# Wide and narrow matmuls of neighbouring products put together in experts 1 to 7

## The chip, the cores and the metric

One core of one Trainium2 chip runs the whole kernel. The metric is the device time in microseconds (us): the median of three runs is 570.77 us (570.52 to 570.80). TensorE (PE) multiplies, VectorE (DVE) and ScalarE (ACT) prepare operands and read results out, GpSimd (POOL) and SyncE (SP) mainly issue transfers.

## The reference

A batch of 512 rows with 1024 features goes through eight experts of three layers, a softmax gate per task, and two small towers:

```python
h = relu(einsum('bi,eio->beo', x, eW1) + eb1)      # 8 experts, 1024 -> 1024
h = relu(einsum('beh,eho->beo', h, eW2) + eb2)     # 1024 -> 512
expert_out = einsum('beh,eho->beo', h, eW3) + eb3  # 512 -> 256
gates = softmax(einsum('bi,tie->bte', x, gW) + gb)
tin = einsum('bte,bed->btd', gates, expert_out)    # 2 tasks
th = relu(tin @ tW1 + tb1); th = relu(th @ tW2 + tb2)   # per task
out = sigmoid(th @ tW3 + tb3)
```

Everything is float32, and the result has to be near float32.

## The kernel before

**Precision.** Each float32 operand is split into a high part (a rounding that PE can read in one pass, `fp32r`) and a low part, the rest. ACT writes the high parts (`w_hi`), DVE the low parts (`w_lo` = raw minus high). A product is then high x high + high weights x low data + low weights x high data. In layers 2 and 3 and the towers these are three matmuls of 512 columns (`triple`, L379 to L382; L380, L381, L382 in the profile).

**Layer 1.** Experts 1 to 7 and half of expert 0 compute layer 1 by a Strassen-Winograd scheme with seven products, P1 to P7, in place of eight. The 1024 outputs are cut into four pairs of two column blocks of 128 (pair 0 to 3). For each pair, `product` (L524) runs one product: four *wide* matmuls (L537: weights `w_hi`, moving data the high and low halves of x or of a sum of x blocks, 2 x 256 = 512 columns), then four *narrow* ones (L540: weights `w_lo`, 256 columns). The last narrow one raises the semaphore `slot_used`, so whoever waits for the product or for its weight slot waits for its narrow part.

**Order on PE.** `pair(e, i)` (L544) gives P1, P2, P5, P6, then P4 of the pair before, P3, P7. Between them stand waits: P6 waits until ACT has copied P1's sum out of PSUM (`n1_taken`, L570), P4 waits for `lower_summed` (L589), P3 until ACT has copied P5 (`p5_taken`, L578), P7 until ACT has copied P6 (`n2_taken`, L582). After pair 3 come layer 3 of the expert before (`layer3`, 24 matmuls; its second half waits for `upper_done` of pair 3, L644), P4 of pair 3, and layer 2 (96 matmuls). PE, ACT and DVE each have this program as a hardware loop over experts 1 to 6, and once more unrolled for expert 7 (`LAST`), where pair 3 is followed by layer 2 at once.

**Order on ACT.** ACT works strictly in its written order (L980 to L1025). The lines that matter are
- `g1_hi` (L822): high parts of the weights of P1, P2, P5 of one pair; `g3_hi` (L850) those of P3 and P7; `g4_hi` (L857) that of P4, into a slot that an earlier product must have left
- `n1_take` (L864), `n2_take` (L871), `p5_take` (L878): the copies out of PSUM of the sums after P1, P6, P5; `p5_take` also waits for `lower_done`
- `c21_take` (L889): reads the result of P4; `pair_h1` (L894): the pair's hidden values.

In pair 0 the order is `g4_hi(0)`, `n1_take(0)`, `g1_hi(1)`, `p5_take(0)`, `g3_hi(1)`, `n2_take(0)`; in pair 2 it is `n1_take(2)`, `p5_take(2)`, `g4_hi(2)`, `g1_hi(3)`, `n2_take(2)`, `c21_take(1)`.

**Order on DVE.** DVE too keeps its written order (L1399 to L1464). `g4_lo(2)`, `sum2(3)`, `sum4(3)`, `g1_lo(3)` follow each other; `g1_lo(3)` releases P1 of pair 3 (`slot_ready`). After `g4_lo(3)` come `c12_sum(2)` (L1213), `upper_fold(2)` (L1228), `lower_fold(2)` (L1241, releases `lower_done`), `c11_sum(3)` (L1207), `w3_lo`, `c21_fold(2)` (L1247, waits for `c21_take(2)`), `w2_lo(0)`, `pair_h1_lo(2)` (L1156, waits for ACT's `pair_h1(2)`), `c12_sum(3)`, `upper_fold(3)`. Low parts of weights are all on L1140.

Of the kernel before, what the change touches and what calls it, by code (L numbers as in the profile page):

```python
# [13 lines left out]
P = 128  # L14
# [68 lines left out]
FIRST_PAIR = 2  # L83
# [62 lines left out]
def nth(e, i):  # L146

    return PAIRS * (e - 1) + i + (PAIRS - FIRST_PAIR)
# [36 lines left out]
def slot_of(product):  # L185
    return USER[product] % RING


def moe_towers(nc, xT, eW1_first, eW1_pairs, eW2, eW3, tW1, tW2, small, out):
    with ExitStack() as ctx:  # L190
# [12 lines left out]
        w_hi, w_lo = sb("w_hi", [RING, SLOT], F32R), sb("w_lo", [RING, SLOT], F32R)  # L203
# [10 lines left out]
        banks = [psum[:, b * BATCH:(b + 1) * BATCH] for b in range(8)]  # L214
# [60 lines left out]
        def halved(x):  # L275
            return x.rearrange("p (n b) -> p n b", n=2)
# [209 lines left out]
        def _(pe):  # L486
# [34 lines left out]
                        pe.matmul(banks[BANK_GROUP[m]][:], w[:, PIECE_SLOT[0], m * P:(m + 1) * P], x[:, 0, :],  # L521
                                  start=(n == 0), stop=False)

            def product(e, p, i):  # L524
                bank_of_pair, source, kh, xh, starts, ends = PRODUCTS[p]
                slot = slot_of((p, i))
                whole = halved(banks[bank_of_pair[i]])
                both = x_both if source == "x" else t_both

                def weights(w, kk):  # L530
                    return w[:, slot, kk * P:(kk + 1) * P]

                def moving(kk):
                    return both[:, :, kh * KK + kk, xh * HALF:(xh + 1) * HALF]

                for kk in range(KK):
                    pe.matmul(whole, weights(w_hi, kk), moving(kk), start=(starts and kk == 0), stop=False,  # L537
                              skip_group_check=True)
                for kk in range(KK):
                    mm = pe.matmul(whole[:, 0, :], weights(w_lo, kk), moving(kk)[:, 0, :], start=False,  # L540
                                   stop=(ends and kk == KK - 1), skip_group_check=True)
                mm.then_inc(slot_used, 1)

            def pair(e, i):  # L544
                first = isinstance(e, int) and e == 0

                if i == PAIRS - 1 and not first:
                    pe.wait_ge(combined, nth(e, 0) + 1)
                elif i == 1:
                    pe.wait_ge(h2_staged, K3 * e)  # L550
                pe.wait_ge(slot_ready, split(e, "G0" if first else "G1", i))
                product(e, "P1", i)

                if not first and i >= 2:
                    pe.wait_ge(upper_done, nth(e, i) - 1)
                elif first and i == FIRST_PAIR:
                    pe.wait_ge(logitsT_ready, 1)
                elif first:
                    pe.wait_ge(h1_staged, 2)
                product(e, "P2", i)  # L560
                if first:
                    pe.wait_ge(slot_ready, split(e, "G1", i))
                    if i == FIRST_PAIR:
                        pe.wait_ge(t_ready, 1)
                if i == 0:

                    pe.wait_ge(gated_ready, 1 + GATED * (e - 1))
                product(e, "P5", i)

                pe.wait_ge(n1_taken, nth(e, i) + 1)  # L570
                pe.wait_ge(slot_ready, split(e, "G2", i))
                if first and i == FIRST_PAIR:
                    pe.wait_ge(t_ready, 2)
                product(e, "P6", i)
                if i > (FIRST_PAIR if first else 0):
                    last_product(e, i - 1)

                pe.wait_ge(p5_taken, nth(e, i) + 1)  # L578
                pe.wait_ge(slot_ready, split(e, "G3", i))
                product(e, "P3", i)  # L580

                pe.wait_ge(n2_taken, nth(e, i) + 1)  # L582
                if first and i == FIRST_PAIR:
                    pe.wait_ge(t_ready, NX)
                product(e, "P7", i)

            def last_product(e, i):

                pe.wait_ge(lower_summed, nth(e, i) + 1)  # L589
                pe.wait_ge(slot_ready, split(e, "G4", i))  # L590
                if isinstance(e, int) and e == 0:
                    pe.wait_ge(t_ready, NX)
                product(e, "P4", i)

            def layer2(e):
                first, last = isinstance(e, int) and e == 0, isinstance(e, int) and e == LAST
# [123 lines left out]
            for k, t in by_tile(range(KT1), T):  # L720
                pe.wait_ge(slot_ready, split(LAST, "T1", t))
                pe.wait_ge(tin_ready, T * k + t + 1)
                for m in range(KT2):
# [4 lines left out]
                    if k == 0 and t == 1:  # L728
# [3 lines left out]
                    slot, cols = TOWER_SLOT["T1", t] + k, slice(m * P, (m + 1) * P)  # L732
                    mm = triple(pe, banks[bank][:], w_hi[:, slot, cols], w_lo[:, slot, cols],
                                x_hi[:, t * OUT3 + k, :], x_lo[:, t * OUT3 + k, :], k == 0, k == KT1 - 1)
# [8 lines left out]
            for t in range(T):  # L743
                pe.wait_ge(slot_ready, split(LAST, "T2", t))
                for i, (k, m) in enumerate(by_bank(range(KT2), KT1)):
# [4 lines left out]
                    if k == 0:  # L750

                        pe.wait_ge(tower1_staged, 2 * t + m + 1)
                    mm = triple(pe, halved(banks[BANK_TOWER2[t][m]]), *tower2_weights(t, k, m),
                                h1_hi[:, :, t * KT2 + k, :], h1_lo[:, :, t * KT2 + k, :], k == 0, k == KT2 - 1)
# [3 lines left out]
            for h in range(2):  # L758
                pe.wait_ge(tower1_staged, 2 * t + m + 1 + h)
                for k in range(KT2):  # L760
                    mm = triple(pe, banks[BANK_LAST[h]][:, 0:HALF], *tower2_weights(t, k, m),
                                h1_hi[:, h, t * KT2 + k, :], h1_lo[:, h, t * KT2 + k, :], k == 0, k == KT2 - 1)
# [4 lines left out]
            for n, (t, cols) in enumerate([(0, slice(0, BATCH)), (1, slice(0, HALF)), (1, slice(HALF, BATCH))]):  # L767
                pe.wait_ge(folded, n + 1)
                pe.matmul(banks[BANK_FINAL[n]][0:1, cols], ones[:], tail_out[:, t * KT1, cols],  # L769
                          start=True, stop=True).then_inc(final_done, 1)  # L770
# [363 lines left out]
        def _(dve):  # L1134
# [63 lines left out]
            def g4_lo(e, i):  # L1198
                first = slot_of(("P4", i))
                split_lo(split(e, "G4", i), slice(first, first + 1), raw_block(i, A22))  # L1200
# [8 lines left out]
            def c12_sum(e, i):  # L1209

                dve.wait_ge(n2_taken, nth(e, i) + 1)
                dve.wait_ge(slot_used, used(e, ("P3", i)))
                dve.tensor_tensor(upper[:, 1, :, :], halved(banks[Q_BANK[i]]), upper[:, 1, :, :],  # L1213
                                  ALU.add).then_inc(upper_summed, 1)
# [22 lines left out]
            def lower_fold(e, i):  # L1237

                quarter_free(e, i)
                dve.wait_ge(lower_summed, nth(e, i) + 1)  # L1240
                dve.scalar_tensor_tensor(quarter[:, 3, :], lower[:, 0, :], prm_of("b1", e * K2 + MG + i),  # L1241
                                         lower[:, 1, :], ALU.add, ALU.add).then_inc(lower_done, 1)
# [156 lines left out]
            with dve.Fori(1, LAST) as e:  # L1399
                sum2(e, 0)  # L1400
                g1_lo(e, 0)
                sum4(e, 0)
                g2_lo(e, 0)
                g3_lo(e, 0)
                hidden2_lo(e, 0)
                hidden2_lo(e, 1)
                hidden2_lo(e, 2)
                g4_lo(e, 0)
                sum2(e, 1)
                sum4(e, 1)  # L1410
                g1_lo(e, 1)
                g3_lo(e, 1)
                c11_sum(e, 0)
                c22_sum(e, 0)
                g2_lo(e, 1)
                hidden2_lo(e, 3)
                lower_fold(e, 0)
                c12_sum(e, 0)
                c11_sum(e, 1)
                g4_lo(e, 1)  # L1420
                upper_fold(e, 0)
                sum2(e, 2)
                sum4(e, 2)
                g1_lo(e, 2)
                c21_fold(e, 0)
                c12_sum(e, 1)
                g2_lo(e, 2)
                c22_sum(e, 1)
                pair_h1_lo(e, 0)
                upper_fold(e, 1)  # L1430
                lower_fold(e, 1)
                g3_lo(e, 2)
                c11_sum(e, 2)
                g4_lo(e, 2)
                sum2(e, 3)
                sum4(e, 3)
                g1_lo(e, 3)
                c21_fold(e, 1)
                g2_lo(e, 3)
                c22_sum(e, 2)  # L1440
                pair_h1_lo(e, 1)
                g3_lo(e, 3)
                g4_lo(e, 3)
                c12_sum(e, 2)
                upper_fold(e, 2)
                lower_fold(e, 2)
                c11_sum(e, 3)
                w3_lo(e)
                c21_fold(e, 2)
                w2_lo(e, 0)  # L1450
                pair_h1_lo(e, 2)
                c12_sum(e, 3)
                upper_fold(e, 3)
                c22_sum(e, 3)
                gate_output(e, 0)
                lower_fold(e, 3)
                w2_lo(e, 1)
                c21_fold(e, 3)
                gate_output(e, 1)
                pair_h1_lo(e, 3)  # L1460
                w2_lo(e, 2)
                w2_lo(e, 3)
                gate_output(e, 2)
                gate_output(e, 3)  # L1464

            e = LAST
# [41 lines left out]
            pair_h1_lo(e, 1)  # L1508
            g3_lo(e, 3)
            g4_lo(e, 3)  # L1510
            c12_sum(e, 2)
            upper_fold(e, 2)
            lower_fold(e, 2)
            c11_sum(e, 3)
            w2_lo(e, 0)
            c21_fold(e, 2)
# [189 lines left out]
```

## Time and profile before

| | us |
|---|---|
| median of three runs | 570.77 |
| the profiled execution | 571.16 |
| its span, first to last instruction | 569.4 |
| PE matmuls busy | 565.6 (99%) |
| DVE busy | 453.8 (80%) |
| ACT busy | 311.1 (55%) |
| TensorE clock granted | 1.000 of full speed |

The busy time of PE counts every matmul from its start to its modelled end, and neighbouring ones overlap. The distance from one start to the next is what a matmul costs in a stream; the timeline gives it. The third expert of the loop is taken as the example below: its P1 of pair 0 starts at 205.28 us.

### The profile page before, as it was taken

The numbers are of one execution on the slowest core, as the hardware profiler recorded it, in microseconds if no ns is written. First come the engines' busy times: TensorE is split into PE (matmuls) and PEld (weight loads), VectorE is DVE, ScalarE is ACT, GpSimd is POOL, SyncE is SP. The second block draws the span as 40 slices with busy tenths as digits, with TensorE's granted clock in tenths as the row PEclk, the third lists the DMA queues.
The fourth block names the chain that finished last, engine by engine and source line by source line (L and its number), as shares of the span: only waits on it lengthen the run. The fifth ranks groups of instructions, "written<-read, shape, count | busy, mean of one in ns | idle before, by whom it ended". The sixth has DMA issues, their size and how long they took to land.

```text
span 569.4 us, 8432 instructions
## 1 busy us (share of the span) xinstructions
PE 565.6 (99%) x2883; PEld 477.6 (84%) x2883; DVE 453.8 (80%) x580; ACT 311.1 (55%) x422; POOL 93.8 (16%) x102
## 2 busy tenths in 40 slices
PE   9999999999999999999999999999999999999998
PEld 6788888888888888888888888888888888888886
DVE  7998579975997769976799759978699767986795
ACT  3584566535663375733665356633757346663644
POOL 0201311052102411033200431024110331100000
PEclk9999999999999999999999999999999999999999
DMA  9727676467726675466744577266654667535000
GB/s 329 212 62 218 151 225 144 147 162 180 178 77 184 189 163 128 147 166 172 197 101 163 145 200 178 79 181 192 161 129 147 166 171 199 149 130 185 0 1 1
DMA packets 39779, 86.94 MB, mean 153 GB/s; under 512 B 3521, under 2 KB 8769, under 8 KB 39762
## 3 DMA queue, kind: packets, MB, share of 16 engines
q1 hardware_dynamic: 29762, 66.50, 34.7%
q0 software_dynamic: 9856, 19.96, 20.9%
q10 hardware_dynamic: 144, 0.26, 0.2%
q8 instruction: 9, 0.15, 0.1%
q14 instruction: 8, 0.07, 0.0%
HBM read 86.68 MB, written 0.04 MB: 152 GB/s over the span
## 4 chain that ended last, share of the span: by engine, by line
PE 98%; ACT 1%; DVE 0%; issue 0%; ACTq 0%
PE psum L537 34%; PE psum L540 17%; PE psum L380 15%; PE psum L381 15%; PE psum L382 15%; PE psum L701 1%; PE psum L521 1%; PE psum L678 0%; ACT scratch L790 0%; ACT scratch L1130 0%; PE psum L769 0%; DVE h_lo L1156 0%; DVE w_lo L1140 0%; ACT w_hi L835 0%; PE psum L687 0%
## 5 line engine op out<-in xcount | busy, mean ns | idle before, releaser
L1140 DVE TENSOR_TENSOR w_lo<-w_raw,w_hi 128x1024 fp32r<-128x1024 f32 (+2 forms) x108 | 135.5, 1255 | 26.3 <-ACT w_hi L857 12.3
L537 PE MATMUL psum<-t_both,w_hi 128*128 128x512 f32 x480 | 130.8, 394 | 0.0
L380 PE MATMUL psum<-h_hi,w_hi 128*128 128x512 f32 (+1 forms) x332 | 128.6, 387 | 0.0
L381 PE MATMUL psum<-h_lo,w_hi 128*128 128x512 f32 (+1 forms) x332 | 128.5, 387 | 0.0
L382 PE MATMUL psum<-h_hi,w_lo 128*128 128x512 f32 (+1 forms) x332 | 128.3, 387 | 0.0
L537 PE MATMUL psum<-x_both,w_hi 128*128 128x512 f32 x360 | 98.2, 394 | 0.0
L537 PEld LDWEIGHTS psum<-t_both,w_hi 128*128 128x128 f32 x480 | 82.6, 189 | 11.5
L1626 POOL DMA_DIRECT2D w_raw<-eW_pairs x30 | 26.0, 868 | 344.8 <-DMA w_raw<-eW_pairs 344.8
L540 PEld LDWEIGHTS psum<-t_both,w_lo 128*128 128x128 f32 x480 | 73.7, 189 | 10.2
L1140 DVE TENSOR_TENSOR w_lo<-scratch,w_hi 128x512 fp32r<-128x512 f32 (+1 forms) x60 | 57.1, 952 | 24.4 <-ACT w_hi L850 23.8
L540 PE MATMUL psum<-t_both,w_lo 128*128 128x256 f32 x480 | 76.4, 281 | 0.0
L1156 DVE SCALAR_TENSOR_TENSOR h_lo<-scratch,h_hi 128x512 fp32r<-128x512 f32 (+1 forms) x62 | 63.3, 1022 | 15.1 <-ACT scratch L930 12.3
L382 PEld LDWEIGHTS psum<-h_hi,w_lo 128*128 128x128 f32 x332 | 62.4, 188 | 12.8
L380 PEld LDWEIGHTS psum<-h_hi,w_hi 128*128 128x128 f32 x332 | 62.4, 188 | 12.3
L381 PEld LDWEIGHTS psum<-h_lo,w_hi 128*128 128x128 f32 x332 | 62.4, 188 | 12.1
L537 PEld LDWEIGHTS psum<-x_both,w_hi 128*128 128x128 f32 x360 | 62.1, 189 | 8.8
L540 PEld LDWEIGHTS psum<-x_both,w_lo 128*128 128x128 f32 x360 | 55.2, 189 | 7.6
L540 PE MATMUL psum<-x_both,w_lo 128*128 128x256 f32 x360 | 57.2, 281 | 0.0
L850 ACT ACTIVATE w_hi<-scratch 128x1024 fp32r<-128x1024 f32 x30 | 31.5, 1051 | 32.0 <-PE psum L382 32.0
L822 ACT ACTIVATE w_hi<-w_raw 128x1536 fp32r<-128x1536 f32 x28 | 41.5, 1483 | 13.1 <-PE psum L382 13.1
L894 ACT ACTIVATE h_hi<-scratch 128x1024 fp32r<-128x1024 f32 x30 | 31.8, 1061 | 22.0 <-DVE scratch L1247 22.0
L918 ACT ACTIVATE w_hi<-w_raw 128x1024 fp32r<-128x1024 f32 x32 | 33.5, 1049 | 17.8 <-DMA w_raw<-eW 16.7
(109 smaller groups left out, 605.3 us busy)
## 6 DMA issues: line engine op xcount, KB each, us to landing
w_raw<-eW_pairs SPq DMA_DIRECT2D x30, 768.0 KB, 4.2
w_raw<-eW SPq DMA_DIRECT2D x40, 512.0 KB, 3.9
scratch<-eW_pairs SPq DMA_DIRECT2D x30, 256.0 KB, 4.9
w_raw<-eW_pairs SPq DMA_DIRECT2D x30, 256.0 KB, 5.1
w_raw<-eW_pairs POOLq DMA_DIRECT2D x30, 256.0 KB, 5.0
scratch<-eW_pairs POOLq DMA_DIRECT2D x30, 256.0 KB, 6.5
scratch<-gates_dram POOLq DMA_DIRECT2D x8, 512.0 KB, 5.6
w_raw<-tW SPq DMA_DIRECT2D x4, 512.0 KB, 4.2
```

The lines of the kernel that those rows point to most:

```text
L380: pe.matmul(bank, weights_hi, moving_hi, start=first, stop=False)
L381: pe.matmul(bank, weights_hi, moving_lo, start=False, stop=False)
L382: return pe.matmul(bank, weights_lo, moving_hi, start=False, stop=last)
L537: pe.matmul(whole, weights(w_hi, kk), moving(kk), start=(starts and kk == 0), stop=False, skip_group_check=True)
L540: mm = pe.matmul(whole[:, 0, :], weights(w_lo, kk), moving(kk)[:, 0, :], start=False, stop=(ends and kk == KK - 1), skip_group_check=True)
L822: act.activation(wide(slice(first, first + 3)), raw_block(i, A11, 3), ACT.Copy).then_inc(slot_hi, 1)
L850: act.activation(wide(slice(first, first + 2)), sums[:, at:at + 2, :].rearrange("p s w -> p (s w)"), ACT.Copy).then_inc(slot_hi, 1)
L894: act.activation(pair_of(h1_hi, i), quarter[:], ACT.Relu).then_inc(h1_taken, 1)
L918: act.activation(wide(slice(2 * i, 2 * i + 2)), unit(u), ACT.Copy).then_inc(slot_hi, 1)
L1140: dve.tensor_tensor(wide(w_lo, slots), raw, wide(w_hi, slots).bitcast(F32), ALU.subtract).then_inc(slot_ready, 1)
L1156: return dve.scalar_tensor_tensor(lo, staged, 0.0, hi.bitcast(F32), ALU.max, ALU.subtract)
L1626: pool.dma_start(raw_block(i, A21), blocks_dram(e, i, A22), accum_op=ALU.add) \
```

## The change

`product` is cut into `high` (the four wide matmuls) and `low` (the four narrow ones with the `slot_used` increment). In experts 1 to 7 the wide parts of two neighbouring products run first, then their narrow parts: P1 with P2 in every pair, P5 with P6 in pairs 1 to 3, and P4 (of the pair before) with P3 in pairs 1 to 3. P7, P5, P6 and P3 of pair 0, P4 of pair 3 and all of expert 0 keep their form. The narrow parts finish in the same sequence as before. The waits stand ahead of the wide part of the product that they guard. On DVE, `lower_fold(2)` moves ahead of `c12_sum(2)` and `upper_fold(2)`, in the loop and in the last expert.

```diff
-                product(e, "P1", i)
+                high("P1", i)
+                if first:
+                    low("P1", i)
                 if not first and i >= 2:
                     pe.wait_ge(upper_done, nth(e, i) - 1)
...
-                product(e, "P2", i)
+                high("P2", i)
+                if not first:
+                    low("P1", i)
+                low("P2", i)
...
-                product(e, "P5", i)
+                high("P5", i)
+                if first or i == 0:
+                    low("P5", i)
                 pe.wait_ge(n1_taken, nth(e, i) + 1)
                 pe.wait_ge(slot_ready, split(e, "G2", i))
...
-                product(e, "P6", i)
-                if i > (FIRST_PAIR if first else 0):
-                    last_product(e, i - 1)
+                high("P6", i)
+                if not first and i > 0:
+                    low("P5", i)
+                low("P6", i)
+                with_last = i > (FIRST_PAIR if first else 0)
+                if with_last:
+                    wait_last(e, i - 1)
+                    high("P4", i - 1)
+                    if first:
+                        low("P4", i - 1)
                 pe.wait_ge(p5_taken, nth(e, i) + 1)
                 pe.wait_ge(slot_ready, split(e, "G3", i))
-                product(e, "P3", i)
+                high("P3", i)
+                if with_last and not first:
+                    low("P4", i - 1)
+                low("P3", i)
...
                 g4_lo(e, 3)
+                lower_fold(e, 2)
                 c12_sum(e, 2)
                 upper_fold(e, 2)
-                lower_fold(e, 2)
                 c11_sum(e, 3)
```

## Rows read from the trace of the kernel before

**Rows 1.** The page, part 4: engines' shares of the chain that ended last.
```profile
PE 98%; ACT 1%; DVE 0%; issue 0%; ACTq 0%
```
**Rows 2.** Waits of PE: engine, line, releaser: us in total, times, longest.
```profile
PE psum L701 <- DVE scratch L1297: 1.2, 1, 1.2
PE psum L687 <- ACT scratch L790: 0.3, 1, 0.3
```
**Rows 3.** Timeline of PE, the third looped expert: start us, us, engine, line, operation.
```profile
205.28 1.07 PE L537 MATMUL psum<-x_both,w_hi 128*128 128x512 f32 x4
...
206.66 1.09 PE L537 MATMUL psum<-x_both,w_hi 128*128 128x512 f32 x4
...
223.50 1.09 PE L537 MATMUL psum<-x_both,w_hi 128*128 128x512 f32 x4
...
227.23 0.63 PE L540 MATMUL psum<-t_both,w_lo 128*128 128x256 f32 x4
...
233.32 1.09 PE L537 MATMUL psum<-x_both,w_hi 128*128 128x512 f32 x4
...
243.14 0.40 PE L380 MATMUL psum<-h_hi,w_hi 128*128 128x512 f32 x1
...
245.89 0.39 PE L380 MATMUL psum<-h_hi,w_hi 128*128 128x512 f32 x1
...
248.61 1.07 PE L537 MATMUL psum<-t_both,w_hi 128*128 128x512 f32 x4
249.52 0.64 PE L540 MATMUL psum<-t_both,w_lo 128*128 128x256 f32 x4
249.99 0.40 PE L380 MATMUL psum<-h_hi,w_hi 128*128 128x512 f32 x1
...
271.78 0.39 PE L537 MATMUL psum<-x_both,w_hi 128*128 128x512 f32 x1
```
**Rows 4.** Timeline of PE, narrow triples of the last layer (same columns).
```profile
562.49 0.28 PE L382 MATMUL psum<-h_hi,w_lo 128*128 128x256 f32 x1
...
562.85 0.28 PE L382 MATMUL psum<-h_hi,w_lo 128*128 128x256 f32 x1
```
**Rows 5.** Timeline of ACT, that expert's pair 0; brackets: idle before, releaser.
```profile
206.85 0.63 ACT L857 ACTIVATE w_hi<-w_raw 128x512 fp32r<-128x512 f32 x1 [1.37 <-PE psum L540]
...
207.87 1.48 ACT L822 ACTIVATE w_hi<-w_raw 128x1536 fp32r<-128x1536 f32 x1
209.66 0.60 ACT L878 ACTIVATE scratch<-psum 128x512 f32<-128x512 f32 x1 [0.31 <-PE psum L540]
```
**Rows 6.** Timeline of ACT, pair 2.
```profile
227.90 0.60 ACT L878 ACTIVATE scratch<-psum 128x512 f32<-128x512 f32 x1 [2.21 <-PE psum L540]
228.40 0.62 ACT L857 ACTIVATE w_hi<-w_raw 128x512 fp32r<-128x512 f32 x1
```
**Rows 7.** Timeline of DVE, pair 2.
```profile
229.05 0.69 DVE L1140 TENSOR_TENSOR w_lo<-w_raw,w_hi 128x512 fp32r<-128x512 f32 x1 [0.40 <-ACT w_hi L857]
...
230.99 1.75 DVE L1140 TENSOR_TENSOR w_lo<-w_raw,w_hi 128x1536 fp32r<-128x1536 f32 x1
```
**Rows 8.** Timeline of ACT, pair 3.
```profile
239.15 0.60 ACT L878 ACTIVATE scratch<-psum 128x512 f32<-128x512 f32 x1 [1.14 <-PE psum L540]
```
**Rows 9.** Timeline of DVE, pair 3 and layer 3.
```profile
238.58 0.48 DVE L1241 SCALAR_TENSOR_TENSOR scratch<-scratch,prm 128x256 f32<-128x256 f32 x1
...
241.22 0.42 DVE L1247 TENSOR_TENSOR scratch<-scratch,psum 128x256 f32<-128x256 f32 x1 [0.44 <-ACT scratch L889]
...
244.75 0.75 DVE L1228 SCALAR_TENSOR_TENSOR scratch<-scratch,prm 128x512 f32<-128x512 f32 x1
```
**Rows 10.** Timeline of all engines where PE was held in expert 0.
```profile
37.52 0.71 ACT L790 ACTIVATE scratch<-psum,prm 128x512 f32<-128x512 f32 x1
...
38.37 0.63 PE L687 MATMUL psum<-ident,scratch 128*128 128x128 f32 x4 [0.28 <-ACT scratch L790]
...
38.75 0.48 PE L537 MATMUL psum<-x_both,w_hi 128*128 128x512 f32 x1
```

More of the change, by code:

```diff
@@ L522, in first_tile, with of_product, high, low @@
                                   start=(n == 0), stop=False)
-            def product(e, p, i):
+            def of_product(p, i):
                 bank_of_pair, source, kh, xh, starts, ends = PRODUCTS[p]
-                slot = slot_of((p, i))
-                whole = halved(banks[bank_of_pair[i]])
                 both = x_both if source == "x" else t_both
-                def weights(w, kk):
-                    return w[:, slot, kk * P:(kk + 1) * P]
                 def moving(kk):
                     return both[:, :, kh * KK + kk, xh * HALF:(xh + 1) * HALF]
+                return slot_of((p, i)), halved(banks[bank_of_pair[i]]), moving, starts, ends
+            def high(p, i):
+                slot, whole, moving, starts, ends = of_product(p, i)
                 for kk in range(KK):
-                    pe.matmul(whole, weights(w_hi, kk), moving(kk), start=(starts and kk == 0), stop=False,
+                    pe.matmul(whole, w_hi[:, slot, kk * P:(kk + 1) * P], moving(kk), start=(starts and kk == 0), stop=False,
                               skip_group_check=True)
+            def low(p, i):
+                slot, whole, moving, starts, ends = of_product(p, i)
                 for kk in range(KK):
-                    mm = pe.matmul(whole[:, 0, :], weights(w_lo, kk), moving(kk)[:, 0, :], start=False,
+                    mm = pe.matmul(whole[:, 0, :], w_lo[:, slot, kk * P:(kk + 1) * P], moving(kk)[:, 0, :], start=False,
                                    stop=(ends and kk == KK - 1), skip_group_check=True)
                 mm.then_inc(slot_used, 1)
+            def product(p, i):
+                high(p, i)
+                low(p, i)
             def pair(e, i):
@@ L584, in pair, with wait_last @@
                     pe.wait_ge(t_ready, NX)
-                product(e, "P7", i)
-            def last_product(e, i):
+                product("P7", i)
+            def wait_last(e, i):
                 pe.wait_ge(lower_summed, nth(e, i) + 1)
@@ L592, in last_product @@
                     pe.wait_ge(t_ready, NX)
-                product(e, "P4", i)
+            def last_product(e, i):
+                wait_last(e, i)
+                product("P4", i)
             def layer2(e):
@@ L1510, in _ @@
             g4_lo(e, 3)
+            lower_fold(e, 2)
             c12_sum(e, 2)
             upper_fold(e, 2)
-            lower_fold(e, 2)
             c11_sum(e, 3)
```

## The prediction

> **What bounds the kernel now.** I read the shares of the chain first: PE holds 98% of it [rows 1]. Then the waits of PE: two in the whole run, 1.5 us together, both outside the experts that change [rows 2]. So today no copy, split or load holds PE; time is the number of matmuls times their distance. Two questions follow: does the new order alter the distances, and do the waits between products stay covered. For the first I read PE's timeline, for the second those of ACT and DVE beside it.
>
> **Distances.** In layer 3 and layer 2 a 512-column matmul comes every 0.227 us. In a stream of narrow ones the distance is 0.120 (0.36 for three [rows 4]). Four wide and four narrow at these rates would be 1.387 us. P4 of pair 3, which follows layer 3, takes 1.38 (248.61 to 249.99), and so does P1 of pair 0 (205.28 to 206.66). But the 26 products from 206.66 to 243.14 take 36.48, 1.403 each [rows 3]. So a return from narrow to wide costs about 17 ns. The price is paid by the wide matmuls that follow: the 12 matmuls from 243.14 to 245.89 take 2.75, where 12 x 0.227 is 2.72 [rows 3].
>
> **What the grouping gives back.** One merged pair of products is 8 wide and 8 narrow: 8 x 0.227 + 0.95 + 0.03 for the return = 2.79, against 2 x 1.403 = 2.81. That is 14 ns each, if eight narrow ones leave no larger debt than four. If the debt goes by the number of narrow matmuls it is nothing. If each removed return saves its full mean it is 17. There are 10 merges per expert, 70 in all: 0 to 1.2 us, and I take 1.0 as long as PE is never held.
>
> The Trainium skill, page "TensorE: Matmul & The Clock Gate", section "Back-to-back issue gap", gives a warm distance of columns / 2.4 + 2.5 ns, 216 and 109 ns here, with no term for the order. By it the regrouping gives exactly 0. The trace disagrees, with 227 and 120 ns and 17 ns per return; I go by the trace.
>
> **What the grouping moves.** A product's `slot_used` rises after its narrow part. In a merged pair the second product ends when it did before. The first one (P1, P5, P4) now ends after both wide parts and its own narrow one, so 4 wide matmuls, 0.9 us, later. At the same time the second product's wide part, and the wait ahead of it, comes 0.47 earlier. Everything queued behind a wait for P1, P5 or P4 on ACT moves by 0.9, and what DVE builds on it too. I follow the four places where a wait of PE has little slack, in the expert that starts at 205.28. Three prices are used: a PE result reaches ACT 0.31 after the start of the last narrow matmul (206.54, which is 206.66 less 0.12, to 206.85 [rows 3, 5]); DVE starts about 0.04 after ACT; and ACT and DVE start an instruction about 0.10 before the one before it ends (227.90 + 0.60 to 228.40 [rows 6]). For the restart of PE after a wait the rows have one case: ACT ends at 38.23, the matmul starts at 38.37, and the next wide one takes 0.48 instead of 0.40 [rows 10]. That is 0.14 to 0.22. I take 0.17, with 0.08 and 0.24 as ends.
>
> *1. P3 of pair 0.* P1 now ends its narrow part later: last narrow start 205.28 + 8 x 0.227 + 0.35 = 207.44, before 206.54. `g4_hi(0)` waits for P1's slot and starts at 207.75 instead of 206.85 [rows 5]. Behind it `n1_take(0)` and `g1_hi(1)` follow at once, so `p5_take(0)` starts 1.02 + 1.48 - 0.10 = 2.40 later, at 210.15, and ends at 210.75. Today it had 0.31 idle ahead of it, so it moves by 0.5 only. P3 would start at 205.28 + 2.77 + 2.80 = 210.85. 210.75 + 0.17 is 210.92: held 0.07 (0 to 0.14). P7 behind it has its `n2_take(0)` just in time. The P1 and P2 block saves 0.02, so pair 1 starts 0.05 late.
>
> *2. Pair 1.* `n1_take`, `p5_take` and `g1_hi(2)` each move by about 0.9 against the pair's start and stay ahead of PE by 0.35 or more. The three merges save 0.04.
>
> *3. P1 of pair 3.* This one is the chain that I trust most. P5 of pair 2 had its last narrow start 4.09 after the pair's start (three products less 0.12); now it is 2.80 + 8 x 0.227 + 0.35 = 4.99, so 0.90 later. `p5_take(2)` waited for P5, and `g4_hi(2)` starts right behind it [rows 6]. DVE's `g4_lo(2)` waited 0.40 for that `g4_hi`, and `sum2(3)`, `sum4(3)` and `g1_lo(3)` follow it without a gap, to 232.74 [rows 7]. No idle time is left in this chain to take up 0.90, so `g1_lo(3)` ends at 233.64. P1 of pair 3 starts at 233.32 today, 0.58 behind its weights [rows 3]. Now: 233.64 + 0.17 = 233.81, so 0.49 late (0.40 to 0.56).
>
> *4. The second half of layer 3.* P4 of pair 2 had its last narrow start 6.90 after pair 3's start; now it is 2.80 + 2.79 + 1.81 + 0.35 + a return of 0.03 = 7.78, or 0.88 later. `c21_take(2)` waits for it, `c21_fold(2)` waited 0.44 for that, then come ACT's `pair_h1(2)`, `pair_h1_lo(2)`, `c12_sum(3)` and `upper_fold(3)`, each bound by the one before, to 245.50 [rows 9]. The second half of layer 3 starts at 245.89 [rows 3] and waits for that fold. Now 245.50 + 0.88 + 0.17 = 246.55: 0.66 late (0.57 to 0.73). Expert 7 has no layer 3 there, and the waits of its layer 2 that depend on pair 3 come 5 us later.
>
> **The fold that is moved** removes one such case. `p5_take(3)` waits for `lower_fold(2)`: that ends at 239.06, and `p5_take(3)` starts at 239.15 [rows 8, 9]. With the later `g4_lo(3)` and the old order it would end 6.8 us after the pair's start, where P3 needs it by 6.35. In the new order the fold is done by 4.7, and ACT's own queue sets `p5_take(3)`, at 5.4 to 6.0. Its price is 0.4 us on `upper_fold(2)`, whose readers (`n2_take(3)`, layer 3) come later than that. DMA: the loads that SP issues after a split move by up to 1 us too. They are issued some microseconds ahead of their use and I cost them at nothing; without that cover it would be at most that 1 us per expert.
>
> **Sum.** Later per expert: 0.05 - 0.04 + 0.49 + 0.66 = 1.16 us, six times 7.0. Expert 7: 0.05 - 0.04 + 0.49 - 0.04 = 0.46. Together +7.4 us, with the ends at (0.91 x 6 + 0.3) = 5.8 and (1.41 x 6 + 0.7) = 9.2. The profiled execution took 571.16, 0.4 above the median, so the same sum on the median 570.77 gives 578.2 (576.6 to 580.0). The gain of the grouping all but vanishes in it: from P1 of pair 3 on, PE starts when it is released and not when it is free.
>
> **Rivals.**
> - *All waits stay covered.* Then the order of matmuls alone speaks: 570.77 - 1.0 = 569.8, or 569.6 with the full 17 ns. For it: PE has no wait today. Against it: two chains without idle time, 0.58 and 0.39 ahead of PE, moved by 0.9. It is the case on the other side, and it decides from the point where each release comes less than 0.4 later than today; past that the waits eat the 1.0 at once. 8%, of which most is faster.
> - *The order doesn't matter and the waits stay covered*, as the page's rule has it for the matmuls: 570.8. The 17 ns in the rows speak against it. 3%.
> - *Only one of the two chains bites.* If layer 3 is not held (`upper_fold(3)` in time), 7.4 - 6 x 0.70 = 3.2, so 574.0; if P1 of pair 3 is not held, 7.4 - 7 x 0.53 = 3.7, 574.5. For it: each chain has five links that I take as rigid. 7%.
> - *A knock-on.* P3 of pair 3 has 0.34 of slack after `p5_take(3)`. If `w2_hi(0)` or `w3_split` ahead of it on ACT waits for its load, or P7 of pair 0 and pair 2 are held 0.1 each, another 0.2 to 0.9 per expert: 580 to 584. 7%.
>
> The forecast itself has 75%. As range I take 574.5 to 580.5. Faster by over 0.2% (1.1 us, about what a measurement of this kernel can tell from no change) has 6%, within 0.2% 5%, slower 89%.
>
> **What the changed profile would show.** PE's waits should list a line of `high` behind DVE `w_lo` seven times with about 0.5, and L380 behind DVE's `upper_fold` six times with about 0.6 to 0.7. The period from one looped expert's P1 to the next, 66.50 today (205.28 to 271.78 [rows 3]), should be near 67.66. `p5_take(2)` should start 5.3 after its pair, not 4.4. A merged block should take 2.79; 2.81 would say that the debt goes by narrow matmuls. The prediction is wrong if the period is below 66.6 or if PE is held in pair 3 at P3.

## The result, and the profile after

The changed kernel takes 579.16 us (median of 4 runs, 578.88 to 579.50) against 570.78 in the same comparison: ratio 1.0143, 95% interval 1.0131 to 1.0155, so 8.4 us slower. 578.2 was forecast, with a range of 574.5 to 580.5. The profiled execution took 579.38, its span is 577.6, and the TensorE clock was again 1.000.

The shares of the chain that ended last, and the waits of PE (engine, line, releaser: us in total, times, longest), of the kernel after:

```profile
PE 87%; DVE 6%; issue 4%; ACT 2%; ACTq 0%; DVEq 0%
```

```profile
PE psum L380 <- DVE scratch L1257: 2.5, 6, 0.4
PE psum L538 <- DVE w_lo L1169: 1.5, 7, 0.3
PE psum L730 <- DVE scratch L1326: 1.2, 1, 1.2
PE psum L716 <- ACT scratch L819: 0.3, 1, 0.3
```

The share of PE in that chain falls from 98% [rows 1] to 87%, while DVE goes from 0% to 6%, "issue" from 0% to 4% and ACT from 1% to 2%. The two old waits of PE are still there (1.2 and 0.3 [rows 2]). Two are new, one six times and one seven times: L380, the triple of layer 3, behind DVE's L1257 (`upper_fold`), and L538, a wide part, behind DVE's L1169 (low parts of weights). The totals of 2.5 and 1.5 us are only the time in which PE had nothing in flight, so they are smaller than the loss. That is read from the starts. PE's timeline after, third looped expert (it starts at 207.94, before at 205.28):

```profile
207.94 1.98 PE L538 MATMUL psum<-x_both,w_hi 128*128 128x512 f32 x8
209.75 1.11 PE L545 MATMUL psum<-x_both,w_lo 128*128 128x256 f32 x8
210.70 1.09 PE L538 MATMUL psum<-t_both,w_hi 128*128 128x512 f32 x4
...
213.53 1.19 PE L538 MATMUL psum<-x_both,w_hi 128*128 128x512 f32 x4
...
216.44 2.00 PE L538 MATMUL psum<-x_both,w_hi 128*128 128x512 f32 x8
...
219.23 2.00 PE L538 MATMUL psum<-t_both,w_hi 128*128 128x512 f32 x8
...
226.22 2.02 PE L538 MATMUL psum<-x_both,w_hi 128*128 128x512 f32 x8
...
229.02 2.00 PE L538 MATMUL psum<-t_both,w_hi 128*128 128x512 f32 x8
...
234.60 1.16 PE L538 MATMUL psum<-t_both,w_hi 128*128 128x512 f32 x4
...
236.42 2.14 PE L538 MATMUL psum<-x_both,w_hi 128*128 128x512 f32 x8 [0.20 <-DVE w_lo L1169]
...
239.34 2.00 PE L538 MATMUL psum<-t_both,w_hi 128*128 128x512 f32 x8
...
246.32 0.40 PE L380 MATMUL psum<-h_hi,w_hi 128*128 128x512 f32 x1
...
249.66 0.50 PE L380 MATMUL psum<-h_hi,w_hi 128*128 128x512 f32 x1 [0.41 <-DVE scratch L1257]
...
252.56 1.07 PE L538 MATMUL psum<-t_both,w_hi 128*128 128x512 f32 x4
...
275.72 0.62 PE L538 MATMUL psum<-x_both,w_hi 128*128 128x512 f32 x2
```

The times in the next sentences are counted from the start of the expert, and those of before from [rows 3]. The wide part of P1 of pair 3 begins at 28.48, before at 28.04; the second half of layer 3 at 41.72, before at 40.61; the next expert at 67.78, before at 66.50. Over the six looped experts the mean period is 67.74 (from 72.48 to 478.91), so +1.24 each. A merged block takes 2.79 to 2.80 (216.44 to 219.23, where the P5/P6 block begins, and 226.22 to 229.02), the one that follows the wide matmuls of layer 2 takes 2.76 (207.94 to 210.70), and eight narrow ones take 0.95 (209.75 to 210.70).

ACT after, pair 0 and pair 2:

```profile
210.42 0.63 ACT L886 ACTIVATE w_hi<-w_raw 128x512 fp32r<-128x512 f32 x1 [2.27 <-PE psum L545]
...
212.82 0.59 ACT L907 ACTIVATE scratch<-psum 128x512 f32<-128x512 f32 x1
```

```profile
231.53 0.60 ACT L907 ACTIVATE scratch<-psum 128x512 f32<-128x512 f32 x1 [2.19 <-PE psum L545]
232.02 0.62 ACT L886 ACTIVATE w_hi<-w_raw 128x512 fp32r<-128x512 f32 x1
```

`g4_hi(0)` starts 2.48 after the expert, before 1.57 [rows 5]. `p5_take(0)` has no idle time left ahead of it and ends at 213.41, 0.12 before P3's wide part (213.53). `p5_take(2)` starts 5.31 after its pair, before 4.40 [rows 6].

DVE after, pair 2:

```profile
232.68 0.69 DVE L1169 TENSOR_TENSOR w_lo<-w_raw,w_hi 128x512 fp32r<-128x512 f32 x1 [0.77 <-ACT w_hi L886]
...
234.62 1.75 DVE L1169 TENSOR_TENSOR w_lo<-w_raw,w_hi 128x1536 fp32r<-128x1536 f32 x1
```

`g4_lo(2)` waits 0.77 where it waited 0.40 [rows 7]. The chain behind it is as dense as before and ends at 236.37. PE starts P1 at 236.42.

ACT and DVE after, pair 3 and layer 3:

```profile
241.97 0.58 ACT L907 ACTIVATE scratch<-psum 128x512 f32<-128x512 f32 x1
...
244.82 0.47 ACT L918 ACTIVATE scratch<-psum,prm 128x256 f32<-128x256 f32 x1 [1.33 <-PE psum L545]
```

```profile
240.82 0.48 DVE L1270 SCALAR_TENSOR_TENSOR scratch<-scratch,prm 128x256 f32<-128x256 f32 x1
...
245.33 0.42 DVE L1276 TENSOR_TENSOR scratch<-scratch,psum 128x256 f32<-128x256 f32 x1 [0.80 <-ACT scratch L918]
...
248.86 0.75 DVE L1257 SCALAR_TENSOR_TENSOR scratch<-scratch,prm 128x512 f32<-128x512 f32 x1
```

`lower_fold(2)` now runs at 240.82, before `p5_take(3)` at 241.97, and no releaser stands beside `p5_take(3)`; before, they stood 0.09 apart [rows 8, 9]. P7 of pair 2 (234.60) takes 1.16 for its wide part where an unheld one takes 1.09: ACT's `n2_take(2)`, the copy that it waits for, ends only 0.10 ahead of it. `c21_take(2)` (L918) starts 8.40 after pair 3, before 7.40 (at 240.72 in that trace). `c21_fold(2)` waits 0.80 for it where it waited 0.44 [rows 9], and `upper_fold(3)` ends at 249.61. The second half of layer 3 starts at 249.66.

### The profile page after: what moved, and what is told of

It reads as the page before. It is cut to its first block, busy times and chain, and to the rows that moved or that the text cites. A ratio compares the mean times of both kernels' runs of the same rounds, so it can differ in the third digit from the quotient of the medians.

```text
span 577.6 us, 8432 instructions
## 1 busy us (share of the span) xinstructions
PE 569.8 (99%) x2883; PEld 478.7 (83%) x2883; DVE 452.1 (78%) x580; ACT 310.3 (54%) x422; POOL 93.7 (16%) x102
## 3 DMA queue, kind: packets, MB, share of 16 engines
q1 hardware_dynamic: 29762, 66.50, 34.1%
## 4 chain that ended last, share of the span: by engine, by line
PE 87%; DVE 6%; issue 4%; ACT 2%; ACTq 0%; DVEq 0%
PE psum L538 29%; PE psum L380 14%; PE psum L381 14%; PE psum L382 14%; PE psum L545 14%; DVE w_lo L1169 4%; DVE scratch L1206 1%; DVE scratch L1257 1%; ACT w_hi L886 1%; DVE scratch L1242 1%; PE psum L730 1%; PE psum L521 1%; ACT scratch L918 1%; PE psum L707 0%; ACT scratch L819 0%
## 5 line engine op out<-in xcount | busy, mean ns | idle before, releaser
L1169 DVE TENSOR_TENSOR w_lo<-w_raw,w_hi 128x1024 fp32r<-128x1024 f32 (+2 forms) x108 | 135.2, 1253 | 40.0 <-ACT w_hi L886 21.3
L380 PE MATMUL psum<-h_hi,w_hi 128*128 128x512 f32 (+1 forms) x332 | 129.2, 389 | 2.5 <-DVE scratch L1257 2.5
L538 PE MATMUL psum<-t_both,w_hi 128*128 128x512 f32 x480 | 127.5, 394 | 0.0
L538 PE MATMUL psum<-x_both,w_hi 128*128 128x512 f32 x360 | 94.3, 396 | 1.5 <-DVE w_lo L1169 1.5
L538 PEld LDWEIGHTS psum<-t_both,w_hi 128*128 128x128 f32 x480 | 84.1, 189 | 12.9
L538 PEld LDWEIGHTS psum<-x_both,w_hi 128*128 128x128 f32 x360 | 65.2, 188 | 15.9 <-DVE w_lo L1169 2.5
L545 PEld LDWEIGHTS psum<-t_both,w_lo 128*128 128x128 f32 x480 | 70.7, 189 | 8.1
L1169 DVE TENSOR_TENSOR w_lo<-scratch,w_hi 128x512 fp32r<-128x512 f32 (+1 forms) x60 | 57.1, 951 | 25.0 <-ACT w_hi L879 24.6
L380 PEld LDWEIGHTS psum<-h_hi,w_hi 128*128 128x128 f32 x332 | 62.4, 188 | 17.1 <-DVE scratch L1257 5.0
L545 PE MATMUL psum<-t_both,w_lo 128*128 128x256 f32 x480 | 72.9, 281 | 0.0
L545 PE MATMUL psum<-x_both,w_lo 128*128 128x256 f32 x360 | 52.8, 281 | 0.0
L545 PEld LDWEIGHTS psum<-x_both,w_lo 128*128 128x128 f32 x360 | 50.0, 190 | 3.4
L918 ACT ACTIVATE scratch<-psum,prm 128x256 f32<-128x256 f32 x30 | 14.2, 474 | 54.8 <-PE psum L545 54.8
```

Of the source, the lines that this page charges most:

```text
L380: pe.matmul(bank, weights_hi, moving_hi, start=first, stop=False)
L538: pe.matmul(whole, w_hi[:, slot, kk * P:(kk + 1) * P], moving(kk), start=(starts and kk == 0), stop=False, skip_group_check=True)
L545: mm = pe.matmul(whole[:, 0, :], w_lo[:, slot, kk * P:(kk + 1) * P], moving(kk)[:, 0, :], start=False, stop=(ends and kk == KK - 1), skip_ ...
L918: act.activation(quarter[:, 1, :], halved(banks[N_BANK[i]])[:, 0, :], ACT.Identity, bias=bias, scale=-1.0).then_inc(c21_taken, 1)
L1169: dve.tensor_tensor(wide(w_lo, slots), raw, wide(w_hi, slots).bitcast(F32), ALU.subtract).then_inc(slot_ready, 1)
```

## The experiments

Two theories stood against each other. By the *release theory* the loss is made by the later end of the first product of a merged block, in three places of which each belongs to one kind of block. By the *matmul theory* the blocks of eight are dearer on PE in themselves. All ratios are to the kernel before on the same chip, which took 571.00 us beside the first four kernels and 571.05 beside the last three. The period is the time from P1 of one looped expert to P1 of the next, 66.50 in the kernel before.

**One kind of block at a time.** The same edit for each of the three, with the other two kinds in their old form. Three small functions say of each kind whether it is merged; in each kernel one of them is always true and the other two are false. The later `low` of each block, not shown, gets the opposite condition:

```diff
-                if first:
+                if first or not merge12(e, i):
                     low("P1", i)
...
-                if first or i == 0:
+                if first or i == 0 or not merge56(e, i):
                     low("P5", i)
...
-                    if first:
+                    if first or not merge43(e, i):
                         low("P4", i - 1)
```

*P1 and P2 only.* 

> Only P1 and P2 are put together (28 blocks in seven experts); P5/P6 and P4/P3 keep their old form, the fold stays moved. Release theory (the loss is the later end of the first product of a merged block): only P3 of pair 0 is held, 0.12 us in each of seven experts, less 28 x 0.014: +0.4 us, 571.2. Matmul theory (blocks of eight are dearer in themselves, 8.4 us over 70 blocks): 28 x 0.12 = +3.4, 574.1, with no hold in the waits of PE.

Measured: 571.31 us, ratio 1.0009 (0.9999 to 1.0018). PE's timeline of this kernel, third looped expert:

```profile
204.95 1.98 PE L538 MATMUL psum<-x_both,w_hi 128*128 128x512 f32 x8
...
210.55 1.19 PE L538 MATMUL psum<-x_both,w_hi 128*128 128x512 f32 x4
...
271.54 0.84 PE L538 MATMUL psum<-x_both,w_hi 128*128 128x512 f32 x3
```

The period is 66.59, 0.09 over that of before. P3 of pair 0 begins 5.60 after the expert. Its four wide matmuls take 1.19, where a group that isn't held takes 1.09: the first distance is 0.10 longer. The list of waits has nothing new in the experts, since matmuls of the product before are still in flight. That is the release theory's size, and the whole +0.3 us lies near the noise of the runs; the matmul theory is 2.8 us off.

*P5 and P6 only.* 

> Only P5 and P6 are put together in pairs 1 to 3 (21 blocks). Release theory: P5 of pair 2 ends 0.9 later, P1 of pair 3 is held by g1_lo(3) in seven experts, 0.55 each, layer 3 is not held: 3.8 - 0.3 = +3.5, 574.3. Matmul theory: 21 x 0.12 = +2.5, 573.3, without a hold.

Measured: 574.50, ratio 1.0062 (1.0045 to 1.0078). The waits of PE:

```profile
PE psum L538 <- DVE w_lo L1178: 1.5, 7, 0.3
PE psum L739 <- DVE scratch L1335: 1.2, 1, 1.2
PE psum L538 <- ACT scratch L916: 0.9, 1, 0.9
PE psum L725 <- ACT scratch L828: 0.3, 1, 0.3
```

The wait of L538 behind DVE is there seven times, and the one of L380 is not. (The 0.9 behind ACT is in expert 0; see the last section.) The period is 67.00, +0.50.

*P4 and P3 only.* 

> Only P4 and P3 are put together in pairs 1 to 3 (21 blocks). Release theory: P4 of pair 2 ends 0.9 later, the second half of layer 3 is held by upper_fold(3) in six experts and not in expert 7, 0.66 each, P1 of pair 3 is not held: 4.0 - 0.3 = +3.7, 574.5. Matmul theory: +2.5, 573.3, without a hold and the same in expert 7.

Measured: 575.10, ratio 1.0077 (1.0061 to 1.0094). The waits of PE:

```profile
PE psum L380 <- DVE scratch L1266: 2.5, 6, 0.4
PE psum L739 <- DVE scratch L1335: 1.2, 1, 1.2
PE psum L725 <- ACT scratch L828: 0.3, 1, 0.3
```

Here L380 waits six times, for `upper_fold`, and L538 never. The period is 67.23, +0.73, and in expert 7 the time from its P1 to its layer 2 is 37.83, where it was 37.86. The matmul theory would have put the same cost there. The three parts add 0.3 + 3.5 + 4.1 = 7.9 us, against 8.4 for all together.

**The fold put back.** The changed kernel with the old order on DVE:

```diff
                 g4_lo(e, 3)
-                lower_fold(e, 2)
                 c12_sum(e, 2)
                 upper_fold(e, 2)
+                lower_fold(e, 2)
```

> The changed kernel with lower_fold(2) put back behind upper_fold(2). If the moved fold covers P3 of pair 3, as forecast: lower_fold(2) ends 1.5 us later, p5_take(3) ends 0.9 later and P3 of pair 3 is held 0.66 in seven experts, with all behind it: +4.6, 583.8. If the fold is off the path: 579.2 as the changed kernel.

Measured: 583.38, ratio 1.0220 (1.0203 to 1.0237), 4.2 us over the changed kernel (4.0 if each is set against the kernel before beside it), and a period of 68.41, 0.67 over that of the changed kernel. ACT and PE, pair 3 of an expert that starts at 208.52:

```profile
243.44 0.60 ACT L907 ACTIVATE scratch<-psum 128x512 f32<-128x512 f32 x1 [0.82 <-DVE scratch L1270]
```

```profile
244.17 1.18 PE L538 MATMUL psum<-x_both,w_hi 128*128 128x512 f32 x4 [0.39 <-ACT scratch L907]
```

`p5_take(3)` idles 0.82 behind L1270, `lower_fold`, and P3 of pair 3 is held behind it; the list of waits has L538 behind L907 seven times, once per changed expert. So the moved fold does cover that place.

**The fold alone**, the same move in the kernel before: 

> The kernel before with only lower_fold(2) moved ahead of c12_sum(2). In the kernel before P3 of pair 3 had 0.6 us of slack behind p5_take(3) and PE had no wait; the move gives slack and takes 0.4 from upper_fold(2), whose readers come later: no change, 570.8 within 0.1%. If the move is a cost by itself (upper_fold later, then layer 3): up to 0.4 x 6 = +2.4, 573.2.

Measured: 571.10, ratio 1.0003 (0.9993 to 1.0012), a period of 66.50 and no new wait. It costs nothing and brings nothing where nothing else is moved.

**What a return from narrow to wide costs.** The kernel before, with the two loops of `product` made one:

```diff
                 for kk in range(KK):
                     pe.matmul(whole, weights(w_hi, kk), moving(kk), ...)
-                for kk in range(KK):
                     mm = pe.matmul(whole[:, 0, :], weights(w_lo, kk), ...)
```

> The kernel before with wide and narrow alternating one by one inside every product (all experts); each product ends when it did, so no wait moves. If the price is per return from narrow to wide (17 ns): three more returns in each of 210 products, +10.7 us, 581.5. If it goes by the number of narrow matmuls: no change, 570.8.

Measured: 572.99, ratio 1.0033 (1.0022 to 1.0045), +1.9 us. Both prices were wrong. PE's timeline of this kernel (L537 wide, L539 narrow):

```profile
207.10 0.28 PE L539 MATMUL psum<-x_both,w_lo 128*128 128x256 f32 x1
207.22 0.40 PE L537 MATMUL psum<-x_both,w_hi 128*128 128x512 f32 x1
207.46 0.28 PE L539 MATMUL psum<-x_both,w_lo 128*128 128x256 f32 x1
207.58 0.40 PE L537 MATMUL psum<-x_both,w_hi 128*128 128x512 f32 x1
...
208.28 0.40 PE L537 MATMUL psum<-t_both,w_hi 128*128 128x512 f32 x1
```

Three wide and three narrow take 1.06 (207.22 to 208.28), 0.353 for one of each, where 0.227 + 0.120 is 0.347. So against these two rates a return costs 7 ns with one wide matmul after it, about 15 ns with four (1.403 against 1.388), and 15 to 25 ns with eight (2.79 to 2.80 against 2.776). The debt is neither one price per return nor one per narrow matmul. The wide ones that follow pay it, at 1 to 9 ns each; the last section has the distances.

**The blocks whose delay is covered.** All merges but P1/P2 of pair 0 and P4/P3 of pair 3, and on ACT:

```diff
                 n1_take(e, 2)
-                p5_take(e, 2)
                 g4_hi(e, 2)
                 g1_hi(e, 3)
+                p5_take(e, 2)
```

> The merged blocks whose delay is covered: all but P1/P2 of pair 0 and P4/P3 of pair 3 (56 blocks), and ACT does g4_hi(2) and g1_hi(3) ahead of p5_take(2). Release theory: no wait of PE is left, only the saved returns from narrow to wide, 56 x 0.014 = -0.8 us: 570.0. Matmul theory: 56 x 0.12 = +6.7, 577.5. If the debt of a return goes by the number of narrow matmuls: 570.8.

Measured: 570.38, ratio 0.9991 (0.9982 to 1.0000). The waits of PE, and its P1 of pair 0 in two experts that follow each other:

```profile
PE psum L739 <- DVE scratch L1335: 1.2, 1, 1.2
PE psum L538 <- ACT scratch L916: 0.9, 1, 0.9
PE psum L725 <- ACT scratch L828: 0.4, 1, 0.4
```

```profile
205.90 1.07 PE L538 MATMUL psum<-x_both,w_hi 128*128 128x512 f32 x4
...
272.32 0.62 PE L538 MATMUL psum<-x_both,w_hi 128*128 128x512 f32 x2
```

The period is 66.42 where it was 66.50: 56 blocks give 7 x 0.08 = 0.6 us, 10 ns each. This version is ahead of the changed kernel, and ahead of the kernel before by an amount at the edge of what the runs can tell. The waits in L380 and L538 behind DVE are gone although 56 of 70 blocks are merged, which the matmul theory excludes (577.5).

## Why the prediction was right

*The grouping itself.* 14 ns for a merged block were forecast, with 0 and 17 as the ends. A block shows 2.79 where two products took 2.81, and the kernel with 56 covered blocks kept 10 ns of each. It was a small term of the right sign. The forecast's own sum, 8 x 0.227 + 0.95 + 0.03, is 2.796 against 2.806, which gives these 10 ns and not the 14 that it states. Its 17 ns per return is taken against computed rates; its own rows have 1.38 for a product behind wide matmuls and 1.403 for one behind narrow ones, 23 ns. In the changed kernel nearly all of it is lost, as said: PE starts when it is released.

*Place 1, P3 of pair 0.* The hold was forecast at 0.07 (0 to 0.14), and pair 1 0.05 late. It was 0.12 and 0.11. `p5_take(0)` ended 5.47 after the expert, exactly as worked out (210.75 is 5.47 after 205.28). What was off is the restart, the one mis-sized term of this place: from the end of `p5_take(0)` at 213.41 to the matmul it is 0.12, and that one takes 0.10 longer than an unheld one, 0.22 together where 0.17 was used. In the trace the instruction that is held here is not the weight load, as at places 3 and 4, but a computation on PE's sequencer for the count of the next wait (`slot_ready` of P3); it runs at 213.44, and the weight load follows 0.09 later. P3 of pair 3 in the kernel without the fold has the same form and nearly the same price, 0.13 + 0.10. That the computation is the reason fits both, but no run takes it away.

*Place 3, P1 of pair 3.* `g1_lo(3)` ends 10.15 after pair 2, and 9.24 + 0.90 = 10.14 was forecast. P1 starts 0.05 later with a first distance of 0.34 in place of 0.23, so 0.16 for the restart against 0.17. (The sum in the prediction, 2.80 + 8 x 0.227 + 0.35, is 4.97 and not 4.99; it leaves out the return of 0.03 that place 4 writes down.) With what it inherits from place 1 it is 0.55 late; 0.50 was forecast. The kernel with P5/P6 alone shows that this hold belongs to those blocks.

*Place 4, the second half of layer 3.* The sum gave 1.16 after all four places; the trace gives 41.72 + 0.11 - 40.61 = 1.22. `upper_fold(3)` ends 249.61 - 236.42 = 13.19 after P1's first start and 13.08 after the point from which PE runs on at its pace (0.11 later), where 12.18 + 0.88 = 13.06 was forecast. The kernel with P4/P3 alone shows this hold in six experts and not in the seventh. The restart costs more than its first distance here: the 12 matmuls of the second half take 2.90 (249.66 to 252.56) and 2.86 in the mean of the six experts, before 2.72 (245.89 to 248.61 [rows 3]), so 0.14 of which 0.11 is counted above.

*The moved fold.* Forecast: `p5_take(3)` done 6.8 after the pair's start without the move, where P3 needs it by 6.35, so with the restart about 0.6 late; and ACT's own queue in charge with it. Measured without it: the copy ends at 7.06 (244.04, where P1 of the pair starts at 236.98), the period grows by 0.67, and the time by 4.0 to 4.2 us over seven experts. With it, ACT's queue is in charge. One reading was wrong: the readers of `upper_fold(2)` were said to come later than its delay, but ACT's `n2_take(3)` now idles 0.33 behind it. It costs nothing, since `c21_take(2)` behind it on ACT still idles 1.33 for P4.

*The sum.* Forecast +7.4: 1.16 six times and 0.46. Measured in the profiled executions: 1.24 six times, 0.6 for expert 7 and what follows, and 0.2 that the start and expert 0, which the change doesn't touch, happened to take longer; together 8.2. Of the 0.8 us missing, 0.4 is the mis-sized term, the restart at place 1, 0.06 in each of seven experts; 0.2 is that start, and 0.02 per looped expert is the part of the restart in layer 3 that goes beyond its first distance. Less than 0.1 in and after expert 7 has no cause that the traces show. (The upper end of the sum adds up to 1.37 per expert and not 1.41, which would lower the 580.0 by 0.2.)

*The signs.* The waits came seven and six times, the period is 67.74 where 67.66 was forecast, and `p5_take(2)` starts 5.31 after its pair. The sizes in the list of waits are smaller than the 0.5 and 0.6 to 0.7 that were named, 0.3 and 0.4 at most: the list counts only time with nothing in flight, while the starts show 0.49 and 0.7.

*The rivals.* Covered waits (569.8) and the order-free rule (570.8) fall with the new waits. "Only one chain bites" falls with the changed kernel's list, which has both, and with the two kernels that show one each. Of the knock-on, one part came, at no price: P7 of pair 2 is held by about 0.06 in every changed expert (its first distance is 0.30 instead of 0.23), but P1 of pair 3 behind it waits for its weights anyway. The part that would cost didn't come: nothing holds P3 of pair 3 in the changed kernel. The kernel without the fold shows what that would cost.

## What to carry to other kernels

A regrouping on a full engine is free only as far as its semaphores allow: the first member of a merged pair tells its readers later by the length of the second, here 0.9 us, and every in-order queue that has a reader of it at its head moves with it. So before two operations are put together, follow each semaphore of the first one through the queues of its readers until idle time takes up the shift. A chain that already ends less than the shift ahead of the full engine will hold it. Where such a chain exists, leave that one block alone, or let the reader's queue do its other work first. Here the two together turned +8.4 us into about -0.6, with an interval that just reaches zero.

## What the runs showed of the hardware

A 512-column matmul in this precision takes 227 ns in a stream of its kind and a 256-column one 120 ns. After narrow ones the wide ones are slower for a while. In layer 2 of the kernels before and after, behind P4 of pair 3, the starts stand 233 or 234, 236, 228, 232 and 231 ns apart, and 227 from there on. How long it lasts depends on more than the last few matmuls: in the covered version a merged block behind four narrow ones has eight slow distances (235, 233, 236, 224, 231, 236, 228, 232, with one short one among them) and takes 2.80, one behind eight narrow ones has five and takes 2.79, and the changed kernel's first block, behind wide ones, takes 2.76 with none. The same slow distances come after a hold too (335 or 341, then for instance 231, 236, 228, 233, 231), with no narrow matmul near, so they are not a price of the width alone. Alternating one by one costs 7 ns a pair. Which part of the engine is behind this stays open. The Trainium skill, page "TensorE: Matmul & The Clock Gate", section "Back-to-back issue gap", gives 216 and 109 ns by its formula, which it calls the gap of an isolated matmul, 131 ns at 512 columns as the sustained figure of a stream, and no term for the order of widths. The runs show 227 and 120 ns and a price for the order, and they decide.

A wait of PE that ends late costs more than the gap to the next start: the first matmul starts 0.05 after its releaser, but the distance to the one behind it is 0.33 to 0.34 instead of 0.23. The matmuls behind those are slower as well, so a hold ahead of layer 3's second half costs 0.14 after its first start, and not 0.11. The list of waits shows 0.2 to 0.3 and 0.4 us for holds whose price in the starts is 0.5 and 0.7, and nothing at all for the 0.12 of pair 0.

Expert 0, which the change leaves alone, has two lengths: to the P1 of expert 1 it takes 42.75 us in the traces of before and after and 44.1 in those of P5/P6 alone and of the covered version, these two with a wait of 0.9 of PE behind ACT's `p5_take`. Why it comes in some executions and not in others stays open. The covered version's eleven runs lie at 570.1 to 570.7 or at 571.3 to 571.4, which fits two such lengths. That spread is more than the gain it was made for, which is why its period in the looped experts is the better proof than its median.
